# A three-layer graph network with routed experts on one core: edge tables made inside the first node sweep, table fills issued by ScalarE, and two steps of node sweeps two and three put in another order

## The reference

```python
def _gat_layer(x, W, attn_l, attn_r, bias, src, dst, num_heads, head_dim, use_elu):
    z = (x @ W).reshape(N, num_heads, head_dim)
    el = jnp.sum(z * attn_l, axis=-1)
    er = jnp.sum(z * attn_r, axis=-1)
    e = jax.nn.leaky_relu(el[src] + er[dst], NEG_SLOPE)
    ex = jnp.exp(e - segment_max(e, dst)[dst])
    alpha = ex / segment_sum(ex, dst)[dst]
    out = segment_sum(alpha[:, :, None] * z[src], dst) + z + bias
    return elu(out) if use_elu else out
# x = x + three such layers (12 heads of 64, 12 of 64, 1 of 768) of layernorm(x)
# x = x + experts(layernorm(x)): top 2 of 8, gelu between two products
```

## Time and profile before

| | us |
|---|---|
| median of 3 runs | 2769.32 |
| lowest, highest | 2766.47, 2769.54 |
| the profiled execution | 2764.62 |
| its span in the trace | 2762.9 |

### The profile page before, as it was taken

How to read it: one execution, slowest core, us unless ns; L and a number is a source line. 1 busy time by engine, 2 the same in 40 slices (tenths; PEclk the granted TensorE clock), 3 DMA queues, 4 the chain that set the end, 5 groups by cost and what they waited for, 6 DMA issues and landing times.

```text
span 2762.9 us, 52272 instructions
## 1 busy us (share of the span) xinstructions
PE 2569.3 (93%) x13226; PEld 1802.1 (65%) x13229; DVE 2077.0 (75%) x4184; ACT 1164.7 (42%) x2481; POOL 1473.7 (53%) x1528
## 2 busy tenths in 40 slices
PE   2997999999999979999999999799999997679998
PEld 1886666666668866666666688555656665467776
DVE  6776999999997769999999877466666666843332
ACT  1223566665654445665666544222322224511111
POOL 1003777777731147777777321577777772124443
PEclk9998999999999989999999999899999998889999
DMA  6446999999968879999999678799999999957776
GB/s 215 167 162 198 341 351 347 351 342 341 343 215 210 209 224 336 358 338 347 350 337 342 216 211 221 234 336 338 335 337 340 337 339 342 359 128 148 147 145 115
DMA packets 199341, 763.40 MB, mean 276 GB/s; under 512 B 41889, under 2 KB 58033, under 8 KB 198542
## 3 DMA queue, kind: packets, MB, share of 16 engines
q0 software_dynamic: 127632, 604.14, 66.4%
q1 hardware_dynamic: 53790, 108.21, 13.0%
q10 hardware_dynamic: 17760, 48.79, 4.5%
HBM read 640.01 MB, written 133.45 MB: 280 GB/s over the span
## 4 chain that ended last, share of the span: by engine, by line
PE 75%; DVE 8%; DMA 6%; POOL 3%; issue 3%; ACT 2%; SPq 2%; ACTq 0%; DVEq 0%; POOLq 0%
PE PS L1065 48%; PE PS L984 8%; PE PS L1188 5%; PE PS L986 4%; PE PS L1177 4%; DMA arena<-table,src_k 3%; POOL arena L677 2%; PE PS L1038 2%; SPq L498 2%; PE PS L1161 1%; PE PS L969 1%; DMA W<-table,src_k 1%; DVE arena L1349 1%; DVE arena L1371 1%; DVE arena L1370 1%
## 5 line engine op out<-in xcount | busy, mean ns | idle before, releaser
L677 POOL DMA_INDIRECT arena<-table,src_k x945 | 928.9, 983 | 299.0 <-issue 212.9
L1065 PE MATMUL PS<-arena,S 128*128 128x384 f32 x2016 | 724.2, 500 | 3.1 <-DVE arena L1512 3.1
L1512 DVE TENSOR_TENSOR arena<-arena,PS 128x768 f32<-128x768 f32 x630 | 579.3, 944 | 0.9 <-ACT arena L827 0.9
L1065 PEld LDWEIGHTS PS<-arena,S 128*128 128x128 f32 x2016 | 374.9, 191 | 212.9 <-issue 8.7
L1065 PE MATMUL PS<-arena,S_weighted 128*128 128x384 f32 x1008 | 352.3, 494 | 8.4 <-DVE S_weighted L1518 8.4
L677 POOL DMA_INDIRECT W<-table,src_k x300 | 295.1, 984 | 94.4 <-issue 65.8
L623 POOL DMA_DIRECT2D table<-arena x75 | 41.5, 554 | 560.6 <-DVEq L1393 384.6
L835 ACT ACTIVATE apart<-iota_row,dst_k 128x128 f32<-128x128 f32 x830 | 260.3, 389 | 4.9 <-PE PS L1065 0.3
L1065 PE MATMUL PS<-parts,S 128*128 128x384 f32 x996 | 241.5, 364 | 21.1 <-DVE parts L1538 14.4
L1065 PEld LDWEIGHTS PS<-arena,S_weighted 128*128 128x128 f32 x1008 | 186.4, 191 | 111.3 <-issue 10.4
L1065 PE MATMUL PS<-W,S 128*128 128x396 f32 (+1 forms) x640 | 232.5, 496 | 0.0
(11 more groups left out here) (295 smaller groups left out, 4394.1 us busy)
## 6 DMA issues: line engine op xcount, KB each, us to landing
arena<-mixed SPq DMA_DIRECT2D x63, 384.0 KB, 3.6
table<-arena POOLq DMA_DIRECT2D x50, 396.0 KB, 3.3
local_b<-local SPq DMA_DIRECT2D x123, 160.0 KB, 6.0
mixed<-sums ACTq DMA_DIRECT2D x50, 384.0 KB
arena<-table SPq DMA_DIRECT2D x50, 384.0 KB, 4.6
arena<-table,src_k POOLq DMA_INDIRECT x945, 5.9
table<-arena POOLq DMA_DIRECT2D x25, 384.5 KB, 4.6
out<-last_bias POOLq DMA_DIRECT2D x25, 384.0 KB, 6.3
```

What stands on the lines that cost most here:

```text
L677: nc.gpsimd.indirect_dma_start(edge_row(l, k % U)[:, 0:table_width(l)], None, table[l][:, :], bass.IndirectOffsetOnAxis(src_k[:, k:k + 1]. ...
L1065: o = nc.tensor.matmul(flat[:, bass.ds(bank + 512 * c, n)], onehot, row[:, c * HALF:c * HALF + n], start=False, stop=True, skip_group_chec ...
L1512: nc.vector.tensor_tensor(z, z, a, ALU.mult).then_inc(s_msg, 1)
```

## The change

1. The six fills go from the head of SP's queue to ACT's, behind `WrT` and ahead of the copies L743.
2. On DVE the block numbers (`block_numbers`), the casts of the edge ends (`ends_of_edges`) and the local rows (`local_numbers`) become a last stage of the first node sweep, at blocks 2, 6 and 10. PE turns the edge ends after the sweep (`turn_ends`), DVE's `tables()` follows the sweep, PE no longer waits for `s_tables` ahead of it, and ACT waits for it before the first edge sweep. `bk_f` moves to another place of its tile.
3. In node sweeps two and three, DVE does the first two of four steps of block 1, then finishes block 0, then does the other two.

```diff
@@ SP
-            for l, h in enumerate(HEADS):
-                used = D + (2 * h if h > 1 else h)
-                sp.dma_start(table[l][0:N, used:PITCH], x[:, used - D:PITCH - D]).then_inc(s_filled, 16)
-                sp.dma_start(table[l][N:NPAD, used:PITCH], x[0:NPAD - N, used - D:PITCH - D]).then_inc(s_filled, 16)
@@ ACT
             act.dma_start(WrT[:, :], ffn["Wr"]).then_inc(s_router, 16)
+            for l, h in enumerate(HEADS):
+                used = D + (2 * h if h > 1 else h)
+                act.dma_start(table[l][0:N, used:PITCH], x[:, used - D:PITCH - D]).then_inc(s_filled, 16)
+                act.dma_start(table[l][N:NPAD, used:PITCH], x[0:NPAD - N, used - D:PITCH - D]).then_inc(s_filled, 16)
...
+                if l == 0:
+                    act.wait_ge(s_tables, 1)
                 if H > 1:
                     for g in range(2):
                         one_hots(g, g)
@@ PE: the turning of the edge ends becomes turn_ends()
-                if l == 0:
-                    pe.wait_ge(s_tables, 1)
                 sweep_nodes(pe, [(first_half, 0), (turn_rows(l, lambda q: turned_banks(l, q)), 1), (second_half, 0)])
+                if l == 0:
+                    turn_ends()
@@ DVE
-            augment_first((2, 3, 4))
-            dve.wait_ge(s_rows_k, 16 * 4)
...
-            augment_first((5,))
+            augment_first((2, 3, 4, 5))
...
+            def later_tables(b):
+                if b.n in (2, 6, 10):
+                    {2: block_numbers, 6: ends_of_edges, 10: local_numbers}[b.n]()
...
                 if l == 0:
                     rest_of_W(0, range(KC), 0)
-                    tables()
...
                     begin(first)
-                    begin(second)
+                    begin(second, 0)
                     dve.wait_ge(s_agg, V * l + AHEAD - G)
                     finish(first)
+                    begin(second, 1)
...
                     stages.insert(3, (augment_next, 0))
+                    stages.append((later_tables, 0))
                     sweep_nodes(dve, stages, rolled=False)
+                    tables()
```

More of the change, by code:

```diff
@@ L952, in _, with turn_ends @@
             last.then_inc(s_tk, 1)
[L954 to L960, removed]
+            def turn_ends():
+                pe.wait_ge(s_rows_f, 1)
+                for j in range(2):
+                    for c in range(4):
+                        n = min(P, V - c * P)
+                        last = nc.tensor.transpose(PS[:, 2 + j, c * P:c * P + n],
+                                                   rows_f()[0:n, (2 * c + j) * P:(2 * c + j + 1) * P], ident[0:n, 0:n])
+                last.then_inc(s_turned, 1)
             def turn_rows(l, banks):
@@ L1280, in _ @@
[L1280 to L1283, removed]
-            augment_first((5,))
-            for c in range(4):
-                n = min(P, V - c * P)
-                link(nc.vector.tensor_scalar(local_rows[0:n, c * P:(c + 1) * P], rows_f()[0:n, (2 * c + 1) * P:(2 * c + 2) * P],
-                                             base[0:n, c:c + 1], -1.0, ALU.subtract, ALU.max))
-                nc.vector.tensor_scalar(local_codes[0:n, c * P:(c + 1) * P], local_rows[0:n, c * P:(c + 1) * P], 1.0, P + 1.0,
-                                        ALU.add, ALU.min).then_inc(s_dl, 1)
@@ L1291, in _, with block_numbers @@
-            link(nc.vector.tensor_scalar(own_code[:, :], own[:, :], 1.0, None, ALU.add))
+            augment_first((2, 3, 4, 5))
+            def block_numbers():
+                link(nc.vector.tensor_copy(b_k[0:1, 0:V], bk_f()[0:1, :]))
+                link(nc.vector.memset(b_k[0:1, V:V + 1], NB))
+                starts = b_k[0:1, 0:V].rearrange("o (g j) -> o g j", j=G)
+                link(nc.vector.memset(b_g[0:1, :, :], NB))
+                link(nc.vector.tensor_copy(b_g[0:1, :, 0:1], starts[:, :, 0:1]))
+                link(nc.vector.tensor_copy(b_g[0:1, 0:NG - 1, 1:2], starts[:, 1:NG, 0:1]))
+                blocks, words = bk_f()[0:1, :].rearrange("o (g j) -> o g j", j=G), b_of[0:1, :, 0:G]
+                link(nc.vector.tensor_scalar(words, blocks, float(FREE - 1), None, ALU.add))
+                link(nc.vector.scalar_tensor_tensor(out=words[:, 0:NG - ER_LEAD], in0=blocks[:, ER_LEAD:], scalar=float(LOW),
+                                                    in1=words[:, 0:NG - ER_LEAD], op0=ALU.mult, op1=ALU.add))
+                link(nc.vector.tensor_copy(ends[0:1, 0:NB - 1], enter[0:1, :]))
+                link(nc.vector.memset(ends[0:1, NB - 1:NB], V))
@@ new lines, in ends_of_edges, with local_numbers @@
+            def ends_of_edges():
+                dve.wait_ge(s_rows_k, 16 * 4)
+                three = 3 * 2 * P
+                link(nc.vector.tensor_copy(rows_f()[:, 0:three], rows_f()[:, 0:three].bitcast(I32)))
+                link(nc.vector.tensor_copy(rows_f()[0:tail, three:], rows_f()[0:tail, three:].bitcast(I32)))
+                dve.sem_inc(s_rows_f, 1)
+            def local_numbers():
+                for c in range(4):
+                    n = min(P, V - c * P)
+                    link(nc.vector.tensor_scalar(local_rows[0:n, c * P:(c + 1) * P], rows_f()[0:n, (2 * c + 1) * P:(2 * c + 2) * P],
+                                                 base[0:n, c:c + 1], -1.0, ALU.subtract, ALU.max))
+                    nc.vector.tensor_scalar(local_codes[0:n, c * P:(c + 1) * P], local_rows[0:n, c * P:(c + 1) * P], 1.0, P + 1.0,
+                                            ALU.add, ALU.min).then_inc(s_dl, 1)
+                link(nc.vector.tensor_scalar(own_code[:, :], own[:, :], 1.0, None, ALU.add))
```

31 lines of the change are left out of this document (11 added, 20 removed).

## The result

| | before | after |
|---|---|---|
| median, us | 2769.54 | 2782.27 |
| lowest, highest | 2766.47, 2773.91 | 2778.24, 2784.68 |
| span of the profiled execution | 2762.9 | 2780.6 |

The ratio is 1.0045, with a 95% interval of 1.0034 to 1.0056: the change costs 12.7 us by the medians of five runs each. The forecast was 11.3 us more and 2780.6 us.

The account below looks back on a forecast made before the run. SP's queue, held 28.02 us by table one's small fill, was taken to keep PE idle until 57.84 us. Terms: +10.5 + 0.8 + 0 + 0 = +11.3 us, from 2769.32 to 2780.6 us; range 2772 to 2794.

Parts of the forecast that it names:

- Term 1: Start, SP's queue: four block DMAs go out at about 3 us instead of 51; DVE's 2.29 us wait goes.
- Term 2: DVE ahead of the first sweep: moved steps leave, W lands 1.0 us later, subtractions of W end at 46.1 us.
- Term 3: ACT's queue at the start: six fills hold ACT until 57.6 us; PE starts at 68.3 against 57.84, +10.5 us.
- The two bounds of the small fill: First small fill on ACT: ends at 32.3 us (quiet queue) to 52.4 (crowded), 38.5 taken; +4.3 to +24.4 us.
- the faster rival: ACT's queue takes the six fills without holding the engine: PE starts at 49.1 us, total 2761.4 us; chance 0.14.
- Term 4: First node sweep: block numbers cost PE 0.8 us, casts and local rows are hidden; bounds 0 and 3.25 us.
- Term 5: Passage to the first edge sweep: tables() moves DVE's reduction by about 1.2 us, hidden; 0, bound +1.2 us.
- Term 6: Sweeps two and three: first rows about 0.9 us sooner, but block 2's load sets the pace; gain 0, bound 1.5 together.
- the low end: Rival, ACT's queue: first fill goes out at the pace of a quiet queue, +5.1 us, 2774.4 us; chance 0.12.
- the high end: Rival, ACT's queue: first fill takes the crowded pace, +25.2 us, 2794.5 us; chance 0.08.

Follow-up runs that it names:

- experiment 1: Changed kernel with the six fills back at the head of SP's queue, all else as after: 2768.31 us, ratio 0.9998 to the kernel before.
- experiment 8: experiment 4 with SP waiting for the first layer's W and block numbers made in two pieces, at blocks 2 and 3: 3005.15 us, ratio 0.9957 to before.
- experiment 5: Changed kernel, but SP starts the DMAs of blocks 0 and 1 only when W of all three layers has landed: 3030.76 us, ratio 1.0040 to before.
- experiment 9: Changed kernel, but SP starts the DMAs of blocks 0 and 1 only when all six fills have landed: 3023.97 us, ratio 1.0019 to before.
- experiment 2: Kernel before with only the six fills moved to ACT's queue, nothing else changed: 2784.97 us, ratio 1.0054 to before.
- Experiment 6: Changed kernel with node sweeps two and three back in their old order: 3032.02 us, ratio 1.0050 to before.
- experiment 7: Changed kernel with the six fills behind ACT's six copies of W: 3030.61 us, ratio 1.0037 to before.
- experiment 11: Changed kernel with the six fills started by GpSimd, behind its gathers of the edge ends: 3006.73 us, ratio 0.9959 to before.
- experiment 4: Changed kernel, but SP fills each block's rows inside the first sweep, three small DMAs a block: 2761.83 us, ratio 0.9973 to before.
- experiment 10: experiment 8 with block 0's moments and rows ahead of DVE's subtractions of W: 3004.33 us, ratio 0.9951 to before.
- experiment 3: Changed kernel with no fills at all, tables only as wide as their used columns: 2761.75 us, ratio 0.9971 to before.

## Why the prediction was right, and where its sizes were off

**Term 1, the fills leave SP: right.** The loads of blocks 0 and 1 go out at 3 us, and DVE waits for none of them (the first moments at 67.51 us have no idle time before them).

**Term 2, DVE's work ahead of the sweep: right, with `W` mis-sized.** The first `W` was to land 1.0 us later, 4.0 for the four block DMAs less 3.0 for the fill that leaves. It ended DVE's wait at 16.65 instead of 12.96 in the kernel before, 3.7 later. The step that failed is the credit for the fill. With the fills on SP, DVE's wait for `W` ends at 12.96 (before) and 12.60 (experiment 1); with no fill ahead and SP waiting, at 12.73 (experiment 8): the fill had cost that first part of `W` nothing. The 4.0 alone was a good estimate: experiments 5 and 9, where only the block DMAs wait, give back 4.0 and 3.8.

**Term 3, the fills hold ACT: right, 2.0 us too small.** Its pieces: `WrT` ended at 25.19, for 23.5 forecast, for the reason of term 2. The first big fill took 1.39 us where SP's rows gave 0.9. The small one behind it was held 15.97 us where the estimate gave 14.1; it was 16.0 to 16.5 in four kernels (after, experiments 2, 6 and 9), and 7.25 in experiment 7, where `W` was out of the queue. So `W` ahead in the queue adds some 9 us, where the estimate had 5.2; that its leaving packets make room for the fill's rows was only argued. The other four took 17.2 us for 19.1, since the first small one of them was held 6.96 (6.97 to 7.76 in experiments 2, 5, 6, 7 and 9) instead of 8.9. Together ACT is free at 59.78 for 57.6. From there to the turn it was 10.56 us, forecast 10.7. The two bounds of the small fill, 6.2 us less and 13.9 more, were wide, but the value taken between them was near. That it came so near is in part luck, since a piece too low by 1.9 us (the small fill) stood beside one too high by 1.9 (the other four). The lower bound also began at 22.46 us, without the 1.0 us by which `W` was to be late; with it, it is 5.2 less.

The rule of the Trainium skill (DMA: Bandwidth & Descriptors, Issuing engines are not separate DMA queues), by which an issue is "usually small relative to the DMA itself", fails for this DMA on ACT: 16.0, 7.0 and 8.6 us in the kernel after, and a forecast by it would have been 2761.4. It agrees with the same rows on GpSimd, where an issue took 0.55 to 1.44 us and 4.5 to 9.3 us passed from issue to landing (experiment 11). On SP with 128 rows at a time an issue took 0.66 us (experiment 4; its trace has no landing). In both the kernel comes out within 2.1 us of the faster rival's first turn (51.16 and 49.70; the rival had 49.1).

**Term 4, steps inside the sweep: right.** The timeline of DVE in the kernel after, at block 2:

```profile
99.79 0.36 DVE L1271 CAST b_k<-ST 1x415 int32<-1x415 f32 x1 [0.15 <-DVE arena L1406]
...
104.17 0.90 DVE L1411 TENSOR_TENSOR xT_rest<-PS,S 128x768 fp32r<-128x768 f32 x1
```

The numbers take 3.05 us (their last step ends at 102.84), and the remaining part L1411 has lost its idle time. PE's turns stand 7.16 us apart, but 15.05 us from 93.67 to 108.72 with one between: 0.73 us late, for 0.8 forecast. From there on all are 7.15 or 7.16 us apart as in the kernel before, so blocks 6 and 10 cost nothing. The last product's 13.5 is the first turn's 12.5, this 0.7, and 0.2 between the first and the second turn (8.85 us for 8.63), which the sum didn't have. That interval doesn't follow the change: it was 8.13 to 9.49 us in the twelve kernels other than that of experiment 10, as PE's matmuls turned from the slower to the faster pace sooner or later.

**Term 5, the passage: right, 0 forecast, 0.4 us gained.** The timeline of all engines of the kernel after:

```profile
254.94 1.32 PE L960 MATMUL PS<-ident,ST 128*128 128x128 f32 x8
...
256.60 0.59 DVE L1306 CAST src_k<-PS 128x415 int32<-128x415 f32 x1
```

The cast of `src_k` stands where the earlier trace rows had DVE's reduction, which comes 1.35 us behind it. DVE's first logits still wait for gathered rows, and the first sum is 13.0 us late where the last product is 13.5.

**Term 6, block 0 sooner: right.** The timeline of DVE entering sweep two of the kernel after:

```profile
822.48 0.95 DVE L1426 CAST S<-PS 128x768 fp32r<-128x768 f32 x1
...
829.51 0.96 DVE L1360 TENSOR_TENSOR arena<-arena,den 128x768 f32<-128x768 f32 x1 [0.94 <-DMA arena<-table]
```

From the taking of the turned rows to block 2 it is 7.03 us, for 6.49 in the earlier trace rows, and the wait for the load is 0.94 for 0.39: most of the gain turned into a wait, as the step said. Counted from the last store of sums (809.70 before, 821.96 after), the rows are taken 0.7 us sooner, for 0.9 forecast, and block 2 starts 0.1 us sooner. In sweep three the wait didn't grow but went from 1.38 to 1.21 us, with rows 0.2 us further ahead of block 2. Experiment 6 finds no value that its runs could tell from nothing.

**Sum.** +11.3 forecast, +12.7 measured. With the 2.0 that term 3 lacked the forecast is 13.3, and the end of sweep one shows 13.5; the passages give back a few tenths. Of the rivals, the low end (a quiet queue for the first fill) is out by 15.97 us, the high end (28 us) as well, and the faster one by the table load at 59.81. The faster one had its point of decision right: ACT is to be free by 46.3 us. In experiment 11 it is free at 24.6, and the time falls below before.

## What to carry to other kernels

An instruction that starts a DMA is work of its engine, and its price follows the rows of the DMA more than its bytes: here a load of 128 rows with 384 KB held SP 0.3 to 0.6 us, and a fill of 3125 rows with 500 KB held back what followed it by 7 to 28 us, most where other packets were already queued. Before such an issue moves, ask what else that engine does next and who waits for it; put it on an engine that has nothing due, or cut it by block, where the issues fall under other work. And a transfer that starts early is in front of something: 1.57 MB of block data, needed only at 67 us, delayed `W` by 3.7 us, and a wait on `W` ahead of it made `W` land that much sooner again. For PE that counted where nothing long stood behind `W` (experiment 8, 1.9 us) or where the block data waited for the fills as well (experiment 9, 3.5 us), and not where they fell among the fills (experiment 5).

## What the runs showed of the hardware that was not expected

- GpSimd's queue is held 0.55 to 1.44 us by each of the six fills, ACT's 0.77 to 15.97 and SP's 0.76 to 28.02, for the same rows.
- On ACT as on SP, the time doesn't appear on the large DMA (0.77 to 1.39 us) but on the next one in the queue. `WrT`, with nothing of the fills ahead of it, is held 5.3 us behind `W`, and 8.95 and 8.43 in experiments 8 and 10. Why it is longer in these two stays open.
- The other engines' issues stay short meanwhile: with SP's queue held for 28.02 us, ACT's next six took 0.35 to 0.65 us each (ahead of `WrT`'s 6.36), and with ACT's held for 19.86 us (experiment 5) SP's four took 0.34 to 0.65. The holding is one of a queue. But the queues are not independent: the same small fill, the first, took 22.7 and 28.0 us on SP beside ACT's `W`, and 7.3 on ACT with `W` gone.
- Two of three chips ran the unchanged kernel some 250 us slower, with gathers at 297 GB/s for 345. Ahead of the first edge sweep nothing of it shows: with ACT free of fills, PE's first turn was at 51.34 us on the first chip (experiment 3) and at 51.16 on the third (experiment 11).
- In the first node sweep PE starts slow in every kernel: a matmul of 512 columns takes 0.63 us at first and 0.39 to 0.40 from 2.8 to 6 us after the first product on, with a granted clock of 1.00 in the rows of both. What ends the slow stretch is not shown. A turn that comes sooner can be worth less at the second block, as in experiment 10.
